# Last stage of a four-stage transformer kernel: the next steps' first norms, transposes and first projections in other units

## The chip, the cores and the metric

The kernel runs on one core of one Trainium2 chip. The metric is the device time in microseconds (us), lower is better. The engines named below are PE (matmul), DVE (vector), ACT (scalar and activation functions), POOL (GpSimd) and SP (which here only issues transfers). Each has a queue of its own and works through it strictly in program order; semaphores tie them together.

## What is computed (reference)

Sixteen images of 113 tokens with 192 features go through four stages; the last two matter here. The third is an attention with eight heads and two groups. The last one is this block, cut to what matters:

```python
e  = gelu(ln(x, r_ln) @ r_in_w.T + r_in_b)           # router
g  = mean(e[:, 1:, :], axis=1, keepdims=True)
h1 = gelu(concat([e, broadcast(g)]) @ r_o1_w.T + r_o1_b)
h2 = gelu(h1 @ r_o2_w.T + r_o2_b)
bits = argmax(h2 @ r_o3_w.T + r_o3_b)                # two bits per token
xa = ln(x, ln1);  q, k, v = xa @ wq.T + bq, xa @ wk.T + bk, xa @ wv.T + bv
o  = softmax(q k^T / 4) v, 12 heads;  o = o @ wo.T + bo
h  = x + bits[:, :, 0:1] * o
ff = gelu(ln(h, ln2) @ fc1_w.T + fc1_b) @ fc2_w.T + fc2_b
out = h + bits[:, :, 1:2] * ff
out = out + (one of three low-rank maps of out, chosen by the bits)
```

## The kernel before, in words

All data are float32. `ffn1_phase` works in four steps of four images (`G = 4`, 452 token columns). `steps` (L2142) runs the body for step 0, then a loop over steps 1 and 2 with a register as the step's number, then step 3, then a tail. A body has twelve units, one for each head. What each engine does in a unit is written out by hand in its own `body`: PE at L2299, ACT at L2402, DVE at L2660, POOL at L2487. In the body of step `it` three streams are interleaved: the attention of step `it` (scores, softmax, turn, values), the late part of step `it - 1` (names `late_...`: output projection, residual, MLP, low-rank maps), and the first part of step `it + 1` (names `pre_...`: two norms, transposes, router, q, k and v).

**The attention of a unit.** PE computes the scores of two heads ahead at even units (L2201), into two PSUM banks. DVE takes the maximum and subtracts it (`softmax_in`, L2556 and L2560), ACT takes the exp in place (L2381), PE transposes it (`turn`, L2210) and ACT copies it out (L2406). PE may compute scores for units n + 2 and n + 3 only when DVE has done the softmax input of units n and n + 1, which held the banks. Every four heads there are `values` (L2223), a copy `outputs` on ACT (L2376), a transposition `back` on PE (L2233) and `divide` on DVE (L2580, L2585).

**The first part of a step.** The first norm has no scale and is kept twice: `stat(it, 0, rows(it))` takes mean and variance of the rows in H (L2516, L2520), POOL the power of the variance (`power`, L2454), and `pre_x` (L2537) writes the norm to `xnext`. POOL copies it to `xmid` and later to `x` (`keep_mid`, `keep_last`), for the residual. `pre_stat` (L2542) and `pre_z` on DVE (L2546) norm `xnext` again into `z`. PE's `pre_z` (L1372) transposes `z` into the PSUM tiles Z1 and Z2; ACT (L1439) and DVE (`pre_z_copy`, L1483) copy them out, scaled for the router (r1, r2) and for the attention (xa1, xa2). `pre_qk(it, t)` (L1394) computes q and k of four heads, of three such parts; ACT copies q (L1457), DVE k (`pre_k`, L1497). `pre_features`, `pre_router1` and `pre_router2` (L1375 to L1392) are the router's layers, each with a Gelu on ACT; DVE's `pre_mean` (L1490) stands between the first two. ACT has to load a table whenever it goes from exp to Gelu or back.

**The order around the change.** DVE in a body: unit 0 softmax 2, `late_o`, `stat(it + 1, 0)`; unit 1 softmax 3, `late_hh`; unit 2 softmax 4, statistics of the residual, `pre_x(it + 1)`; unit 3 softmax 5, `pre_stat`, `late_y`; unit 4 softmax 6, `late_y_copy`, `pre_z`; unit 5 softmax 7, `divide`, `pre_z_copy`; unit 6 softmax 8, `pre_mean`; unit 7 softmax 9, `pre_k` 0, `late_mlp` 0; unit 8 softmax 10, `pre_k` 1, `late_mlp` 1; unit 9 softmax 11, `divide`, `late_u`; unit 10 softmax 12, `pre_k` 2, `late_down`; unit 11 softmax 13, `late_d`. Softmax 12 and 13 are those of the next step's heads 0 and 1. PE transposes `z` in unit 5, has router and feature projections of the MLP in unit 6, the three q and k parts in units 7, 8 and 10. POOL takes, in order, `power(it + 1, 0)`, `power(it - 1, 2)`, `power(it + 1, 1)`, the two copies and `out(it - 1)`, the add of the MLP's result to H.

**PSUM tiles of the first part.** The tiles Z1, Z2, R (router features), H1, H2, Q0, K0, ... V1, LG take the banks 4 and 5 in turn; a tile may be filled when the tile two before it has been copied out (`Tiles.free`). The list of readers beside them (L1321) says who copies each.

**The stage before** (`attn1_phase`, body of PE at L1755, ACT at L1857, DVE at L2015) runs, in its last step, the first part of step 0 of the last stage: PE transposes in unit 2, router layers in units 3 to 5, q and k parts in units 6 to 8.

## Time and profile before

| | us |
|---|---|
| median of 3 runs (lowest, highest) | 975.55 (973.28, 978.21) |
| the profiled execution | 979.58 |
| its span, first to last instruction | 977.8 |
| PE, DVE, ACT, POOL busy | 797.9, 495.4, 306.4, 365.4 |
| last stage, step 0 (627.4 to 686.4) | 59.0 |
| step 1 (686.4 to 765.1) | 78.6 |
| step 2 (765.1 to 843.6) | 78.6 |
| step 3 (843.6 to 903.4) | 59.8 |
| the tail, to the end of the span | 74.4 |

A step is counted from its body's first scores; the steps' limits are read from PE's timeline. Steps 1 and 2 are longer than the others because they carry all three streams. In the rows below, a line number is the kernel's line that issued the instruction (for a helper, the helper's), `x16` is how many instructions one row merges, and a bracket gives how long the engine had been idle before and on what it had waited. The granted clock is given as a share of 2.4 GHz, so 0.50 is the 1.2 GHz level and 1.00 the 2.4 GHz level.

### The profile page before, as it was taken

To read this page: it belongs to the slowest core of one execution; us is meant where nothing else is said; L and a number is where in the kernel's file an instruction comes from. 1 tells how busy PE (TensorE), PEld (TensorE's weight loads), DVE (VectorE), ACT (ScalarE), POOL (GpSimd) and SP (SyncE) were. 2 spreads that over 40 slices of the span, in tenths; PEclk is the share of its full clock that TensorE was granted. 3 is DMA by queue.
4 is the path that set the end of the run, shared out by engine and by line. 5 is a ranking of instruction groups with operands and counts; after the bars stand their busy time and mean duration, and the time that the engine had idled before them with its cause. 6 is when DMAs were issued, how large, how long until landed. Compare 5 with 4: busy or idle time off the path is not lost.

```text
span 977.8 us, 14811 instructions
## 1 busy us (share of the span) xinstructions
PE 797.9 (82%) x4860; PEld 572.6 (59%) x4860; DVE 495.4 (51%) x1223; ACT 306.4 (31%) x571; POOL 365.4 (37%) x233
## 2 busy tenths in 40 slices
PE   7988872279999999988979788779799799888572
PEld 4665662147667777756767574554656656656351
DVE  4354655524644444658676965363824743634210
ACT  1121321023333333333424337144352252342200
POOL 3015888786820287758786100010200100000000
PEclk9787765569999999997979899858789879989795
DMA  8831113334543344444111000000000000000000
GB/s 235 238 106 46 35 29 72 68 79 115 119 124 88 87 117 114 103 127 98 35 29 31 1 1 1 1 1 1 2 0 1 14 0 0 13 3 1 15 0 15
DMA packets 81395, 52.96 MB, mean 54 GB/s; under 512 B 42942, under 2 KB 76719, under 8 KB 80305
## 3 DMA queue, kind: packets, MB, share of 16 engines
q1 hardware_dynamic: 27330, 29.82, 10.9%
q0 software_dynamic: 40960, 11.98, 6.8%
q10 hardware_dynamic: 13040, 10.30, 3.7%
q8 instruction: 39, 0.64, 0.3%
q14 instruction: 26, 0.21, 0.1%
HBM read 29.53 MB, written 21.69 MB: 52 GB/s over the span
## 4 chain that ended last, share of the span: by engine, by line
PE 60%; POOL 16%; DVE 9%; issue 6%; ACT 3%; DMA 3%; SPq 0%; DVEq 0%; ACTq 0%; POOLq 0%
POOL work L223 8%; POOL xs_scratch L212 6%; PE ex_up L1143 6%; PE ex_up L1144 6%; PE ps L2270 4%; PE ps L2201 3%; PE ex_yp L1166 3%; PE ex_yp L1167 3%; PE ps L1355 2%; PE ps L1357 2%; PE ps L1350 2%; PE ps L2210 2%; PE ps L1356 2%; PE a_ps L392 1%; PE ps L1366 1%
## 5 line engine op out<-in xcount | busy, mean ns | idle before, releaser
L223 POOL DMA_INDIRECT work<-ys_scratch,place x64 | 153.8, 2403 | 87.5 <-DMA ys_scratch<-ex_yb 57.5
L212 POOL DMA_INDIRECT xs_scratch<-e_t,e_routed x64 | 152.8, 2387 | 43.0 <-issue 29.3
L1242 DVE TENSOR_SCALAR ex_bb<-ex_up 128x384 f32<-128x384 f32 x44 | 24.5, 558 | 118.6 <-PE ex_up L1144 87.7
L1143 PE MATMUL ex_up<-e_wa,ex_x 128*128 x176 | 75.1, 509 | 8.4 <-issue 6.9
L1144 PE MATMUL ex_up<-e_wb,e_ex_x 65*128 x176 | 73.9, 501 | 0.0
L2480 POOL TENSOR_TENSOR H<-H,f_hh 113x768 f32 (+1 forms) x4 | 7.2, 1810 | 146.7 <-DVE f_hh L2623 146.7
L2458 POOL TENSOR_SCALAR f_veps<-f_mv 113x4 f32<-113x4 f32 x10 | 1.9, 194 | 144.8 <-DVE f_mv L2520 144.8
L1201 ACT ACTIVATE ex_sg<-ex_up 128x384 f32<-128x384 f32 x44 | 21.6, 492 | 106.3 <-PE ex_up L1144 96.9
L2406 ACT ACTIVATE f_pT<-ps 113x452 f32<-113x452 f32 x48 | 26.2, 546 | 77.5 <-PE ps L2210 77.4
L1144 PEld LDWEIGHTS ex_up<-e_wb,e_ex_x 65*128 65x128 f32 x176 | 34.4, 196 | 24.7 <-issue 2.1
L2201 PE MATMUL ps<-f_k,f_q 32*113 32x113 f32 x384 | 32.5, 320 | 16.9 <-DVE f_p L2560 15.8
L1143 PEld LDWEIGHTS ex_up<-e_wa,ex_x 128*128 128x128 f32 x176 | 30.9, 195 | 25.7 <-issue 12.8
L1166 PE MATMUL ex_yp<-e_wa,ex_a 128*128 x176 | 43.5, 329 | 0.8 <-ACT ex_yb L1208 0.8
L1167 PE MATMUL ex_yp<-e_wb,e_ex_a 65*128 x176 | 43.3, 327 | 0.0
L2201 PEld LDWEIGHTS ps<-f_k,f_q 32*113 32x113 f32 x384 | 27.6, 221 | 22.0 <-DVE f_p L2560 15.9
L2210 PE MATMUL ps<-ident,f_p 113*113 113x113 f32 x192 | 36.8, 324 | 3.6 <-ACT f_pT L2406 3.6
L2623 DVE SCALAR_TENSOR_TENSOR f_hh<-ps,f_bits,f_hh 113x192 f32<-113x192 f32 x16 | 5.9, 413 | 64.4 <-PE ps L2270 64.4
L2381 ACT ACTIVATE f_p<-f_p 113x452 f32<-113x452 f32 x48 | 27.8, 578 | 32.9 <-DVE f_p L2560 32.5
L1126 PE MATMUL ex_xt<-ident,ex_xb 128*128 128x128 f32 x88 | 22.7, 283 | 17.7 <-DMA ex_xb<-xs_scratch 17.7
L2270 PE MATMUL ps<-fc,f_ff 128*113 128x192 f32 x192 | 36.9, 344 | 0.0
L2210 PEld LDWEIGHTS ps<-ident,f_p 113*113 113x113 f32 x192 | 28.3, 216 | 13.4 <-issue 11.9
L2556 DVE TENSOR_REDUCE f_mx<-ps 113x4 f32<-113x452 f32 x48 | 29.9, 624 | 12.0 <-PE ps L2201 10.8
(372 smaller groups left out, 1921.9 us busy)
## 6 DMA issues: line engine op xcount, KB each, us to landing
ex_xb<-xs_scratch SPq DMA_DIRECT2D x88, 96.0 KB
ys_scratch<-ex_yb ACTq DMA_DIRECT2D x44, 192.0 KB
xs_scratch<-e_zeros SPq DMA_DIRECT2D x62, 96.0 KB
e_wa<-in_wa SPq DMA_DIRECT2D x4, 1152.0 KB
e_wb<-in_wb SPq DMA_DIRECT2D x4, 576.0 KB
e_wa<-in_patches SPq DMA_DIRECT2D x4, 432.0 KB, 9.3
out<-H SPq DMA_DIRECT2D x4, 339.0 KB
w4a<-in_w4a SPq DMA_DIRECT2D x1, 1216.0 KB
```

The lines of the kernel that those rows point to most:

```text
L212: nc.gpsimd.indirect_dma_start(out=dram.xs, out_offset=bass.IndirectOffsetOnAxis(ap=S.pos[:, j, k:k + 1], axis=0), in_=S.t[:, j, :], in_of ...
L223: nc.gpsimd.indirect_dma_start(out=S.yk[:, it % 2, j, k, :], out_offset=None, in_=dram.ys[it // X.steps], in_offset=bass.IndirectOffsetOnA ...
L1143: mm(o, x1[:, p % 3, t], S.wa[:, bass.ds(w, 2 * I)], start=True, stop=False)
L1144: m = mm(o, x2[:, p % 3, t], S.wb[:, bass.ds(w, 2 * I)], start=False, stop=True)
L1166: mm(o, a1[:, p % 2, t], S.wa[:, bass.ds(w, D)], start=True, stop=False)
L1167: m = mm(o, a2[:, p % 2, t], S.wb[:, bass.ds(w, D)], start=False, stop=True)
L2201: m = mm(units.bank(h)[0:N, s], q[r:r + STRIP, h // HQ, s], k[r:r + STRIP, h // HQ, s], start=True, stop=True, tile_position=(r, 0))
L2210: m = nc.tensor.transpose(PT[0:N, j * N:(j + 1) * N], p[:, n % (AHEAD + 1), j, :], S.ident[0:N, 0:N])
L2270: m = mm(o, ff[:, f, j * N:(j + 1) * N], S.fc2[:, f, :], start=False, stop=(f == KF - 1))
L2381: cp(pp, pp, ACT.Exp, scale=float(HD) ** -0.5).then_inc(exp_ok.sem, 1)
L2406: cp(pT[:, n % 5, :, :], PT[0:N, 0:GN], ACT.Copy).then_inc(pt_out.sem, 1)
L2556: nv.tensor_reduce(mx[:, n % 2, :], sc, AX.X, ALU.max).then_inc(mx_ok.sem, 1)
```

## The change

In the last stage the two unscaled norms are made two steps ahead, later in the body. In the first body DVE makes the norms of step 1 where it made them before, and those of step 2 besides: `stat(it + 2, 0)` in unit 5, `pre_x(it + 2)` in unit 6, `pre_stat(it + 2)` in unit 8 and `pre_z(it + 2)` in unit 10. In the middle bodies only the latter stay. For step 2 they read rows of a step that does not exist; `ahead` then points at H's first rows, and the result is not used. As `z` is ready when a middle body begins, PE transposes it in unit 2 for unit 5 and computes the first q and k part in unit 3 for unit 7; ACT and DVE copy there too (DVE: `pre_z_copy` in unit 2 for 5, `pre_k` 0 in unit 3 for 7, ahead of `late_y`). In the first body the transposes stay and the first q and k part goes to unit 6, ahead of the router. The tiles Q0 and K0 take their places in the ring between Z2 and R. In the last step of the stage before, the first q and k part moves from unit 6 to unit 3, the router's three layers from units 3, 4, 5 to 4, 5, 6, and DVE's mean from unit 4 to unit 5. POOL's powers are reordered to match. The bodies of step 3 and the tail have the same instructions as before.

```diff
@@ -1318,7 +1318,7 @@
     F.z_ok, F.gm_ok, F.gs_ok = (counted(nc, ctx, "f_" + n, per) for n, per in (("z_ok", G), ("gm_ok", 1), ("gs_ok", 1)))
-    F.proj = Tiles(nc, ctx, "f_proj", S.bank[4:6], ["act", "dve", "act", "act", "act", "act", "dve", "act", "dve", "act", "dve",
+    F.proj = Tiles(nc, ctx, "f_proj", S.bank[4:6], ["act", "dve", "act", "dve", "act", "act", "act", "act", "dve", "act", "dve",
                                                     "act", "dve", "dve"])
@@ -1329,7 +1329,8 @@
     HEADS, HD, RHD = 12, D // 12, 128
-    Z1, Z2, R, H1, H2, Q0, K0, Q1, K1, Q2, K2, V0, V1, LG = range(14)
+    Z1, Z2, Q0, K0, R, H1, H2, Q1, K1, Q2, K2, V0, V1, LG = range(14)
+    QS, KS = (Q0, Q1, Q2), (K0, K1, K2)
     images, mm, P = four, nc.tensor.matmul, Names()
@@ -1392,9 +1393,9 @@
     def pre_qk(it, t):
-        pe.wait_ge(*proj.free(it, Q0 + 2 * t))
-        pe.wait_ge(*proj.free(it, K0 + 2 * t))
-        mq, mk = two_linear(proj.bank(Q0 + 2 * t)[:, 0:GN], proj.bank(K0 + 2 * t)[:, 0:GN], w.q + 128 * t, w.k + 128 * t, 128,
+        pe.wait_ge(*proj.free(it, QS[t]))
+        pe.wait_ge(*proj.free(it, KS[t]))
+        mq, mk = two_linear(proj.bank(QS[t])[:, 0:GN], proj.bank(KS[t])[:, 0:GN], w.q + 128 * t, w.k + 128 * t, 128,
                             xa1[:], xa2[:])
@@ -1455,7 +1457,7 @@
     def pre_q(it, t):
-        evac(it, proj, Q0 + 2 * t, q[:, t, :], 128, ACT.Identity, bias=col(c.q + t))
+        evac(it, proj, QS[t], q[:, t, :], 128, ACT.Identity, bias=col(c.q + t))
 
@@ -1495,9 +1498,9 @@
     def pre_k(it, t):
-        dve.wait_ge(*done(proj.filled, it, K0 + 2 * t))
-        nv.tensor_scalar(k[:, t, :], proj.bank(K0 + 2 * t)[:, 0:GN], S.c4a[:, c.k + t:c.k + t + 1], None, ALU.add
-                         ).then_inc(proj.out(K0 + 2 * t), 1)
+        dve.wait_ge(*done(proj.filled, it, KS[t]))
+        nv.tensor_scalar(k[:, t, :], proj.bank(KS[t])[:, 0:GN], S.c4a[:, c.k + t:c.k + t + 1], None, ALU.add
+                         ).then_inc(proj.out(KS[t]), 1)
 
@@ -1790,14 +1793,14 @@
                         nxt.pre_z(0, False)
-                    if n == 3 and last:
+                    if n == 4 and last:
                         nxt.pre_features(0)
-                    if n == 4 and last:
+                    if n == 5 and last:
                         nxt.pre_router1(0)
-                    if n == 5 and last:
+                    if n == 6 and last:
                         nxt.pre_router2(0)
-                    if n in (6, 7, 8) and last:
-                        nxt.pre_qk(0, n - 6)
+                    if n in (3, 7, 8) and last:
+                        nxt.pre_qk(0, max(0, n - 6))
                     if n in (2, 8):
@@ -1881,14 +1884,14 @@
                         nxt.pre_z(0)
-                    if n == 3 and last:
+                    if n == 4 and last:
                         nxt.pre_features(0)
-                    if n == 4 and last:
+                    if n == 5 and last:
                         nxt.pre_router1(0)
-                    if n == 5 and last:
+                    if n == 6 and last:
                         nxt.pre_router2(0)
-                    if n in (6, 7, 8) and last:
-                        nxt.pre_q(0, n - 6)
+                    if n in (3, 7, 8) and last:
+                        nxt.pre_q(0, max(0, n - 6))
                 outputs(it, 1)
@@ -2056,10 +2059,10 @@
                         nxt.pre_z_copy(0)
-                    if n == 4 and last:
+                    if n == 5 and last:
                         nxt.pre_mean(0)
-                    if n in (6, 7, 8) and last:
-                        nxt.pre_k(0, n - 6)
+                    if n in (3, 7, 8) and last:
+                        nxt.pre_k(0, max(0, n - 6))
                 if not last:
@@ -2190,8 +2194,8 @@
                 if n % HQ == 0:
-                    pe.wait_ge(*proj.copied(it, Q0 + 2 * (n // HQ)))
-                    pe.wait_ge(*proj.copied(it, K0 + 2 * (n // HQ)))
+                    pe.wait_ge(*proj.copied(it, QS[n // HQ]))
+                    pe.wait_ge(*proj.copied(it, KS[n // HQ]))
                 pe.wait_ge(*units.free(it, n))
@@ -2309,16 +2313,16 @@
                         late_y(it - 1)
-                    if n == 5 and not last:
+                    if n == (5 if first else 2) and not last:
                         pre_z(it + 1)
+                    if n == (6 if first else 3) and not last:
+                        pre_qk(it + 1, 0)
                     if n == 6:
...
                                 (pre_features, pre_router1, pre_router2)[m](it + 1)
-                    if n == 7 and not last:
-                        pre_qk(it + 1, 0)
                     if n == 7 and not first:
@@ -2412,8 +2416,10 @@
                         outputs(it, 0)
-                    if n == 5 and not last:
+                    if n == (5 if first else 2) and not last:
                         pre_z(it + 1)
+                    if n == (6 if first else 3) and not last:
+                        pre_q(it + 1, 0)
                     if n == 6:
@@ -2421,8 +2427,6 @@
                                 (pre_features, pre_router1, pre_router2)[m](it + 1)
-                    if n == 7 and not last:
-                        pre_q(it + 1, 0)
                     if n == 8 and not last:
@@ -2485,17 +2489,19 @@
             def body(it, first, last):
-                if not last:
+                if first:
                     power(it + 1, 0)
-                if not first:
+                    power(it + 1, 1)
+                else:
                     power(it - 1, 2)
-                if not last:
-                    power(it + 1, 1)
                 keep_last(it)
...
                     keep_mid(it + 1)
+                    power(it + 2, 0)
                 if not first:
                     out(it - 1)
+                if not last:
+                    power(it + 2, 1)
 
@@ -2534,10 +2540,10 @@
 
-            def pre_x(it):
+            def pre_x(it, src):
 
                 dve.wait_ge(*done(xmid_ok, it, -1))
-                norm(it, 0, rows(it), xnext, x_ok)
+                norm(it, 0, src, xnext, x_ok)
 
@@ -2658,6 +2664,8 @@
             def body(it, first, last):
+                if not last:
+                    ahead = rows(2 if first else (STEPS - 1) * (2 - it))
                 for n in range(NU):
@@ -2665,40 +2673,51 @@
                         late_o(it - 1)
-                    if n == 0 and not last:
+                    if n == 0 and first:
                         stat(it + 1, 0, rows(it + 1))
...
                         stat(it - 1, 2, hh)
-                    if n == 2 and not last:
-                        pre_x(it + 1)
-                    if n == 3 and not last:
+                    if n == 2 and first:
+                        pre_x(it + 1, rows(it + 1))
+                    if n == 3 and first:
                         pre_stat(it + 1)
+                    if n == 2 and not (first or last):
+                        pre_z_copy(it + 1)
+                    if n == 3 and not (first or last):
+                        pre_k(it + 1, 0)
                     if n == 3 and not first:
...
                         late_y_copy(it - 1)
-                    if n == 4 and not last:
+                    if n == 4 and first:
                         pre_z(it + 1)
+                    if n == 5 and first:
+                        pre_z_copy(it + 1)
                     if n == 5 and not last:
-                        pre_z_copy(it + 1)
+                        stat(it + 2, 0, ahead)
+                    if n == 6 and first:
+                        pre_k(it + 1, 0)
                     if n == 6 and not last:
                         pre_mean(it + 1)
-                    if n == 7 and not last:
-                        pre_k(it + 1, 0)
+                        pre_x(it + 2, ahead)
                     if n == 7 and not first:
...
                         late_mlp(it - 1, 1)
+                    if n == 8 and not last:
+                        pre_stat(it + 2)
                     if n == 9 and not first:
...
                         late_down(it - 1)
+                    if n == 10 and not last:
+                        pre_z(it + 2)
                     if n == 11 and not first:
```

## Rows read from the trace of the kernel before

**Rows 1.** The page's part 4, the chain that ended last, whole kernel.

```profile
PE 60%; POOL 16%; DVE 9%; issue 6%; ACT 3%; DMA 3%; SPq 0%; DVEq 0%; ACTq 0%; POOLq 0%
```

**Rows 2.** Windows of steps 0 and 1: length, busy us by engine, PE clock, DMA share, GB/s.

```profile
627.00:686.00 59.00, 47.70 (x331) 31.20 (x331) 30.91 (x73) 23.73 (x40) 4.91 (x7) 0.68 0.00 1
...
699.00:717.00 18.00, 16.57 (x106) 12.25 (x106) 12.18 (x30) 8.24 (x14) 2.81 (x4) 0.56 0.01 1
```

**Rows 3.** Timeline of step 1, PE and one ACT row; columns: start us, us.

```profile
686.42 1.05 PE L2201 MATMUL ps<-f_k,f_q 32*113 32x113 f32 x16
...
694.83 0.62 PE L2210 MATMUL ps<-ident,f_p 113*113 113x113 f32 x4 [0.73 <-ACT f_pT L2406]
699.61 1.86 PE L2201 MATMUL ps<-f_k,f_q 32*113 32x113 f32 x16 [4.16 <-DVE f_p L2560]
...
712.58 1.74 PE L1355 MATMUL ps<-work,w4a 128*128 128x452 f32 x2
...
716.30 1.17 ACT L1434 ACTIVATE f_ff<-ps,c4a 128x452 f32<-128x452 f32 x2 [0.92 <-PE ps L1358]
...
718.11 1.03 PE L1355 MATMUL ps<-work,w4a 128*128 128x452 f32 x2
...
726.81 1.03 PE L1355 MATMUL ps<-f_xa,w4a 128*128 128x452 f32 x2 [0.28 <-ACT f_h L1434]
...
729.48 0.57 PE L2268 MATMUL ps<-fc2b,ones 1*113 1x192 f32 x2
...
747.69 1.05 PE L2201 MATMUL ps<-f_k,f_q 32*113 32x113 f32 x16
...
758.13 0.58 PE L1366 MATMUL ps<-w4a,work 128*113 128x192 f32 x2 [0.43 <-DVE work L2644]
```

**Rows 4.** Timeline of step 1, DVE.

```profile
689.47 1.12 DVE L2516 BATCH_NORM_STATS2 f_stats<-H 113x6 f32 x4
...
691.03 0.60 DVE L2556 TENSOR_REDUCE f_mx<-ps 113x4 f32<-113x452 f32 x1
...
697.11 1.25 DVE L2526 TENSOR_SCALAR e_x<-H,f_mv,f_rstd 113x192 f32 x4
698.27 0.62 DVE L2556 TENSOR_REDUCE f_mx<-ps 113x4 f32<-113x452 f32 x1
...
710.00 0.74 DVE L1486 TENSOR_SCALAR f_r<-ps,c4b 64x452 f32<-64x452 f32 x1 [1.35 <-PE ps L1350]
...
712.18 0.63 DVE L2556 TENSOR_REDUCE f_mx<-ps 113x4 f32<-113x452 f32 x1
...
745.17 0.63 DVE L2556 TENSOR_REDUCE f_mx<-ps 113x4 f32<-113x452 f32 x1 [0.24 <-DVE f_hh L2623]
```

**Rows 5.** Timeline of step 3, PE and, last, DVE.

```profile
843.62 1.05 PE L2201 MATMUL ps<-f_k,f_q 32*113 32x113 f32 x16
...
855.14 1.86 PE L2201 MATMUL ps<-f_k,f_q 32*113 32x113 f32 x16 [2.58 <-DVE f_p L2560]
...
861.95 0.69 PE L2233 MATMUL ps<-ident,f_ot 128*113 128x128 f32 x4 [0.74 <-ACT f_ot L2376]
...
853.74 0.60 DVE L2556 TENSOR_REDUCE f_mx<-ps 113x4 f32<-113x452 f32 x1
```

**Rows 6.** Timeline of step 0, PE.

```profile
654.19 1.74 PE L1336 MATMUL ps<-f_r,w4a 128*128 128x452 f32 x2
...
666.02 1.41 PE L1355 MATMUL ps<-f_xa,w4a 128*128 128x452 f32 x2
```

**Rows 7.** Timeline of the attention stage's last step, ACT, then PE.

```profile
601.70 1.28 ACT L1434 ACT_TABLE_LOAD   x1
602.99 0.63 ACT L1434 ACTIVATE f_h<-ps,c4a 64x452 f32<-64x452 f32 x1
...
603.77 1.00 PE L1355 MATMUL ps<-f_xa,w4a 128*128 128x452 f32 x2 [0.95 <-ACT f_h L1434]
...
611.02 1.00 PE L1355 MATMUL ps<-f_xa,w4a 128*128 128x452 f32 x2 [0.33 <-DVE f_k L1499]
```

More of the change, by code:

```diff
@@ L1428, in ffn1_pre_scalar @@
     HEADS, HD, RHD = 12, D // 12, 128
-    Z1, Z2, R, H1, H2, Q0, K0, Q1, K1, Q2, K2, V0, V1, LG = range(14)
+    Z1, Z2, Q0, K0, R, H1, H2, Q1, K1, Q2, K2, V0, V1, LG = range(14)
+    QS, KS = (Q0, Q1, Q2), (K0, K1, K2)
     images, cp, P = four, nc.scalar.activation, Names()
@@ L1476, in ffn1_pre_vector @@
     HEADS, HD, RHD = 12, D // 12, 128
-    Z1, Z2, R, H1, H2, Q0, K0, Q1, K1, Q2, K2, V0, V1, LG = range(14)
+    Z1, Z2, Q0, K0, R, H1, H2, Q1, K1, Q2, K2, V0, V1, LG = range(14)
+    QS, KS = (Q0, Q1, Q2), (K0, K1, K2)
     images, nv, P = four, nc.vector, Names()
@@ L2113, in ffn1_phase @@
         units = Tiles(nc, ctx, "f_units", bank[0:2], ["dve"] * NU)
-        Z1, Z2, R, H1, H2, Q0, K0, Q1, K1, Q2, K2, V0, V1, LG = range(14)
+        Z1, Z2, Q0, K0, R, H1, H2, Q1, K1, Q2, K2, V0, V1, LG = range(14)
+        QS, KS = (Q0, Q1, Q2), (K0, K1, K2)
         O1, O2, WO, Y1, Y2, F, FO, U1, U2, DN, D1, D2, UP = 0, 1, 2, 4, 5, 6, 12, 14, 15, 16, 18, 19, 20
```

## The prediction, made before the change was run

> **What bounds the kernel now.** I read the page's chain of waits first, then the last stage by windows, then PE, DVE and ACT of one middle step in order of time. PE holds 60% of the chain [rows 1]; in the last stage it is busy most of the time, but at two clocks. A middle step (step 1, 686.4 to 765.1) has 18 us in which PE is 16.57 us busy at a mean granted clock of 0.56, that is nearly all at the 1.2 GHz level; the rest of it is at 2.4 GHz, step 2 repeats it, and in step 0 the mean clock is 0.68 [rows 2]. The low stretch begins in a hole of PE's work: 0.73 us before the turn of unit 3, then 4.16 us before the scores of heads 6 and 7, released by DVE [rows 3]. DVE is the cause: in units 0 to 3 it carries the previous step's residual and statistics and, for the next step, statistics, a first norm and second statistics [rows 4]. The change takes just these out of units 0 to 3 and gives PE work for the hole.
>
> **Middle steps (1 and 2), units 0 to 3.** Out of DVE's way before softmax 5 go the statistics at unit 0 (689.47 to 691.03, 1.56 us) and the norm at unit 2 (697.11 to 698.27, 1.16 us) [rows 4]. The first comes through only in part, since DVE then waits for PE's products. Step 3 has neither: there softmax 5 starts 10.12 us after the step's first scores (853.74 less 843.62, [rows 5]), in step 1 11.85 us (698.27 less 686.42, [rows 3, 4]). So both are worth 1.7 us. In comes the copy of the transposed norm, 710.00 to 712.18, 2.2 us with its hand-over [rows 4]. In step 1's times it ends at about 698.7, and softmax 5 (a maximum and a subtraction of 0.63 us each) at 699.95: the scores of heads 6 and 7 are free no earlier than at 699.61 now. The stall is filled, not shortened. PE runs the 8 transposes (0.95 us), then waits from 695.5 to 698.7, 3.2 us, for the copy, then runs the first q and k projection: 2.67 us at full clock (726.81 to 729.48, [rows 3]), some 5.1 us at the low one, my estimate by doubling.
>
> Queued behind: DVE's k copy now waits for PE inside unit 3, with the late norm (1.16 us as the other) and softmax 6 behind it. ACT's q copy has behind it only a copy that waits for a later turn of PE anyway.
>
> **Does the clock still fall?** Step 3 has a hole of 2.58 us and falls too, from before its scores at 855.14 (1.86 us) until before 861.95 (0.69 us) [rows 5]. My 3.2 us lies between 2.58 and 4.16, both of which fell, so I take the fall. What follows differs: in step 1 the clock came back only during the feature projections at 712.58, 1.74 us long where their like at 718.11 take 1.03 [rows 3]. Now a projection of the same kind stands right behind the hole. I take a low stretch of about 7 us, as in step 3; its ends are none and today's 15 to 17 us.
>
> With 7 us: projection to 703.8, scores and turn to 705.4, late norm ready at 705.9, its transposes and the values to 707.8, copy, back and turn to 710.3, scores and turn of unit 6 to 711.8, against 712.58 now. Then ACT is late next: softmax 7, divide, the new statistics (1.56 us) and softmax 8 end at 713.6, then an exp, the table load of 1.28 us [rows 7] and two Gelus of 1.17 us together [rows 3] end at 716.7, when the second pair of feature projections may start, now at 718.11 [rows 3]: 1.4 us gained. Unit 7 loses the projection, from the turn's end (726.81 less 0.28) to 729.48 [rows 3]: 3.0 us.
>
> **What comes back on DVE.** The second statistics (1.56 us) stand before softmax 11, which now starts at 745.17 [rows 4]; it ends near 748.05, and the scores now at 747.69 [rows 3] wait 0.4 us. The second norm (1.16 us) stands between the down product and the copy for which PE's last up-projection waits, now until 758.13 [rows 3]; 1.6 us with the 0.4. The norm at unit 6 and the statistics at unit 5 cost nothing beyond the delay of softmax 8 above: PE's router and projections hide them; without that cover they are 1.16 and 1.56 us. POOL's power for the second norm stands behind its add to H, but unit 10 comes 8 us later. Per middle step: 1.4 + 3.0 - 1.6 = 2.8 us gained; 5.2 if the clock holds (features start at 709.2, their second pair at 714.3: 3.8 + 3.0 - 1.6); -0.7 if the low stretch lasts as now (features at 715.5, so 2.1 lost there). Twice 2.8 is 5.6 us.
>
> **Step 0** does two steps' norms, 5.4 us of DVE more, in units 5 to 10. Most hides; the statistics at unit 8 delay softmax 11 and PE's scores by 1.0 us. PE's projection moves from 666.02, where it took 3.1 us, ahead of the features at 654.19, in the low stretch [rows 6]: 5.1 us there if the clock stays low, and the features then wait 0.75 us for ACT's q copy, since they now share its PSUM bank. If the clock comes back during the projection, the features (1.74 us for a pair at the low clock, [rows 6]) and the router run at full clock and the step gains 1.8 net; if not it loses 2.9. I take 0.5 lost. Step 2's norms for a step that does not exist are in the 1.6. **Step 3** and the tail have no moved work: nothing.
>
> **The attention stage's last step.** The projection moves ahead of the router there too. DVE's k copy now blocks softmax 6, and the last router layer goes to unit 6, where ACT runs a table load, an exp and a load again before it can free the bank of the next projection. Each load is 1.28 us, and at 603.77 PE waits 0.95 us for that result today; by my order it waits 2.2 us there, and the third projection starts at 612.05, now at 611.02 [rows 7]: 1.0 us lost. The bounds are 0 (other work covers it) and 2.7 (the new holes of 1.7 and 2.2 us let the clock fall once).
>
> The Trainium skill, in "ScalarE: Activation LUTs", section What ACT_TABLE_LOAD costs, gives a switch 1.283 us of load and some 1.38 us of drain besides. The load agrees: begun at 601.70 it ends before the activation of 602.99 [rows 7], which starts right behind it, so a drain has no room. By the page the two switches in that wait would make it 2.8 us longer and the sum that much worse; I go by the rows.
>
> **Sum.** -5.6 + 0.5 + 1.0, and 1.7 for one clock fall in a new hole (in the attention stage, or before the up-projection in two steps, each about even). A fall costs between nothing and 3.4 us, half of step 3's 6.8 us from 855.14 to 861.95 [rows 5]; I take the middle. That is -2.4 us. The profiled execution took 979.58 us, so 977.2 on its terms; it stands 4.0 above the median of the runs, 975.55, from which I get 973.2.
>
> The Trainium skill, in "TensorE: Matmul & The Clock Gate", Part 1, says that the place of the clock's rise varies from run to run and that the ramp is under 1% of a typical kernel. Here the rows disagree in size: 16.57 us busy at 0.56 [rows 2] is some 7 us per middle step, 14 us or 1.5% in two. By the page's size (a) and (b) would have no price of their own, and the sum would stay near -2.4.
>
> **Rivals.** (a) The filled hole keeps PE at 2.4 GHz. For it: the hole is 1 us shorter than now. Against: step 3's 2.58 us. Price: 2 x 5.2 + 1.8 - 1.0 = 11.2 us, 964.4. Chance 0.17.
> (b) Slower: in unit 3 DVE waits for a projection at the low clock, with the late norm and softmax 6 behind, and the clock does not return before the features. From a low stretch of some 13 us on, this decides. For it: transposes and scores without a pause did not bring the clock back in step 1. Price: 2 x 0.7 + 2.9 in step 0 + 2.7 in the attention stage = 7.0 us, 982.6. Chance 0.18.
> (c) The DVE work moved to units 8 and 10 takes back what the hole gave, by a clock fall before each up-projection: 2 x 1.7 more, 976.6. Chance 0.10, and it is no change.
> My forecast has 0.55. Its own range is 967 to 978.
>
> **Numbers.** A measurement of this kernel can tell 0.5%, 4.9 us. Faster by more: all of (a) and three in ten of the forecast, 0.33. Slower by more: most of (b) and a little of the forecast, 0.18. The rest, 0.49, is no change. The range takes in most of (a) and of (b): 964.5 to 981.
>
> **What would show it.** Right: PE's hole at unit 3 is about 3 us, the scores of heads 6 and 7 start over 3 us later than now, the low stretch of steps 1 and 2 is about 7 us, the steps last about 76 us for 78.6, PE waits some 1.5 us for DVE before the up-projection. Wrong: a clock that never falls there (a), a low stretch until the features (b), a step 0 that changes by over 3 us, or an attention stage that ends earlier.

## The result, and the profile after

| | before | after |
|---|---|---|
| median of 15 runs each, us | 976.45 | 982.4 |
| lowest, highest | 963.67, 986.38 | 971.17, 991.78 |
| span of the profiled execution | 977.8 | 981.7 |

The ratio is 1.0077, interval [1.0039, 1.0114]: slower, where I had forecast 973.2 with a range up to 981.0. The same kernel was timed twice more: 1.0009 [0.9953, 1.0064] (e4_same) and 1.0040 [1.0013, 1.0068] (e12_same_again). The mean of the three is 1.0042, about 4 us slower. A median is over all executions of a kernel, while the ratios leave out the slow ones, those over 1.5% above the kernel's fastest, which is why e5_fill_mid can have a median of 982.17 us and a ratio below 1.

The view by windows, cut where the work changes: from the transposes of the attention stage's last step to the last stage's first scores, then steps 0, 1, 2, then step 3 with the tail. Columns: stretch and length, busy us (and instructions) of PE, PE's weight loads, DVE, ACT, POOL, then PE's granted clock, DMA share, GB/s. Before:

```profile
582.25:627.40 45.15, 35.99 (x260) 22.89 (x259) 19.95 (x37) 23.07 (x34) 0.00 (x0) 0.96 0.00 1
627.40:686.42 59.02, 48.12 (x334) 31.57 (x334) 31.19 (x73) 23.73 (x40) 4.91 (x7) 0.68 0.00 1
686.42:765.05 78.63, 70.40 (x479) 47.87 (x478) 40.33 (x101) 28.02 (x48) 7.02 (x9) 0.89 0.01 1
765.05:843.62 78.57, 70.35 (x480) 47.87 (x479) 40.32 (x101) 28.02 (x48) 7.04 (x9) 0.89 0.01 4
843.62:977.80 134.18, 87.72 (x557) 60.95 (x556) 40.33 (x95) 28.68 (x48) 6.83 (x7) 0.83 0.03 8
```

And after:

```profile
584.90:637.75 52.85, 41.56 (x260) 26.48 (x259) 19.85 (x37) 23.18 (x34) 0.00 (x0) 0.84 0.00 1
637.75:699.49 61.74, 49.13 (x335) 32.59 (x335) 36.25 (x97) 23.72 (x40) 7.30 (x11) 0.70 0.00 1
699.49:773.90 74.41, 65.69 (x479) 43.15 (x478) 40.01 (x101) 27.76 (x48) 7.02 (x9) 0.98 0.01 2
773.90:848.43 74.53, 65.84 (x479) 43.16 (x478) 39.99 (x101) 27.77 (x48) 7.01 (x9) 0.98 0.01 5
848.43:981.70 133.27, 87.10 (x557) 60.43 (x556) 40.18 (x95) 28.65 (x48) 6.80 (x7) 0.83 0.03 8
```

Read the lengths against each other: the attention stage's last step is 7.70 us longer, step 0 2.72 longer, steps 1 and 2 4.22 and 4.04 shorter, step 3 with the tail 0.91 shorter: +1.25 us together. The remaining 2.65 of the span's 3.9 us lie ahead of the transposes (582.25 to 584.90), where both kernels have the same instructions. The clock column says more: with two levels, a stretch of length L at mean clock c has been at 1.2 GHz for 2 x (1 - c) x L. This is called its low time from here on. In a middle step that was 17 us and is 3 us; in the attention step it was 4 us and is 17 us.

Step 1 after, PE, in order of time; it answers [rows 3]:

```profile
699.49 1.05 PE L2205 MATMUL ps<-f_k,f_q 32*113 32x113 f32 x16
...
707.00 0.94 PE L1351 MATMUL ps<-ident,e_z 113*128 113x113 f32 x8
707.89 0.62 PE L2214 MATMUL ps<-ident,f_p 113*113 113x113 f32 x4
711.66 1.88 PE L1356 MATMUL ps<-f_xa,w4a 128*128 128x452 f32 x2 [3.15 <-DVE f_xa L1491]
...
715.84 1.05 PE L2205 MATMUL ps<-f_k,f_q 32*113 32x113 f32 x16
...
723.27 0.94 PE L1356 MATMUL ps<-work,w4a 128*128 128x452 f32 x2
...
728.30 1.02 PE L1356 MATMUL ps<-work,w4a 128*128 128x452 f32 x2 [0.47 <-ACT f_ff L1436]
...
736.65 0.58 PE L2272 MATMUL ps<-fc2b,ones 1*113 1x192 f32 x2
...
755.45 1.05 PE L2205 MATMUL ps<-f_k,f_q 32*113 32x113 f32 x16 [0.52 <-DVE f_p L2566]
...
766.98 0.58 PE L1367 MATMUL ps<-w4a,work 128*113 128x192 f32 x2 [1.52 <-DVE work L2650]
```

The middle step is as drawn in the prediction. PE waits 3.15 us for DVE's copy (forecast 3.2), the projection starts at the low clock (1.88 us for 1.03 in [rows 3]), the scores of heads 6 and 7 come 16.35 us into the step for 13.19 before, and DVE's returned work makes PE wait 0.52 and 1.52 us. But the clock is back within the projection, after 3.4 us and not 7.

The attention stage's last step after, ACT and then PE; it answers [rows 7]:

```profile
606.74 0.55 ACT L1848 ACTIVATE a_ot<-ps 128x452 f32<-128x452 f32 x1 [2.09 <-PE ps L1719]
607.31 1.28 ACT L1436 ACT_TABLE_LOAD   x1
608.60 0.64 ACT L1436 ACTIVATE f_h<-ps,c4a 128x452 f32<-128x452 f32 x1
609.14 0.54 ACT L1864 ACTIVATE a_pT<-ps 113x452 f32<-113x452 f32 x1
609.69 1.28 ACT L1842 ACT_TABLE_LOAD   x1
610.99 0.58 ACT L1842 ACTIVATE a_p<-a_p 113x452 f32<-113x452 f32 x1
611.58 1.28 ACT L1436 ACT_TABLE_LOAD   x1
612.88 0.63 ACT L1436 ACTIVATE f_h<-ps,c4a 64x452 f32<-64x452 f32 x1
```

```profile
610.36 0.65 PE L1693 MATMUL ps<-ident,a_p 113*113 113x113 f32 x4
613.66 1.84 PE L1356 MATMUL ps<-f_xa,w4a 128*128 128x452 f32 x2 [2.65 <-ACT f_h L1436]
...
619.73 1.00 PE L1356 MATMUL ps<-f_xa,w4a 128*128 128x452 f32 x2
```

PE's second projection waits 2.65 us for the Gelu of the last router layer (forecast 2.2), because ACT goes through load, Gelu, copy, load, exp, load, Gelu in strict order. The clock falls in that hole, so it takes 6.07 us from this projection to the next, where 3.63 are needed before (607.39 to 611.02).

### The profile page after: what moved, and what is told of

Read it like the earlier page. It is cut to its first block, busy times and chain, and to the rows that moved or that the text cites. A ratio compares the mean times of both kernels' runs of the same rounds, so it can differ in the third digit from the quotient of the medians.

```text
span 981.7 us, 14847 instructions
## 1 busy us (share of the span) xinstructions
PE 796.8 (81%) x4860; PEld 569.1 (58%) x4860; DVE 499.4 (51%) x1247; ACT 306.1 (31%) x571; POOL 367.2 (37%) x237
## 4 chain that ended last, share of the span: by engine, by line
PE 65%; DVE 14%; POOL 8%; issue 6%; ACT 3%; DMA 2%; SPq 0%; DVEq 0%; ACTq 0%; POOLq 0%
POOL xs_scratch L212 6%; PE ex_up L1143 6%; PE ex_up L1144 6%; PE ps L2274 3%; PE ex_yp L1166 3%; PE ex_yp L1167 3%; PE ps L2205 3%; PE ps L1634 3%; PE ps L1356 2%; PE ps L1358 2%; PE ps L1357 2%; PE ps L1674 2%; PE ps L1613 2%; DVE H L236 1%; PE a_ps L392 1%
## 5 line engine op out<-in xcount | busy, mean ns | idle before, releaser
L1144 PE MATMUL ex_up<-e_wb,e_ex_x 65*128 x176 | 71.9, 489 | 0.0
L2205 PE MATMUL ps<-f_k,f_q 32*113 32x113 f32 x384 | 30.0, 303 | 10.2 <-DVE f_p L2566 9.2
L2214 PE MATMUL ps<-ident,f_p 113*113 113x113 f32 x192 | 34.7, 310 | 2.2 <-ACT f_pT L2410 2.2
L1674 PE MATMUL ps<-a_k,a_q 32*113 32x113 f32 x256 | 21.6, 308 | 16.8 <-DVE a_p L1960 16.8
L2205 PEld LDWEIGHTS ps<-f_k,f_q 32*113 32x113 f32 x384 | 25.5, 205 | 15.7 <-DVE f_p L2566 8.0
```

The source lines that it names most:

```text
L1144: m = mm(o, x2[:, p % 3, t], S.wb[:, bass.ds(w, 2 * I)], start=False, stop=True)
L1674: return mm(units.bank(n)[0:N, c], q[r:r + STRIP, t, c], k[r:r + STRIP, t, c], start=True, stop=True, tile_position=(r, 0))
L2205: m = mm(units.bank(h)[0:N, s], q[r:r + STRIP, h // HQ, s], k[r:r + STRIP, h // HQ, s], start=True, stop=True, tile_position=(r, 0))
L2214: m = nc.tensor.transpose(PT[0:N, j * N:(j + 1) * N], p[:, n % (AHEAD + 1), j, :], S.ident[0:N, 0:N])
```

## Experiments

Lengths are given in the order of the windows above (attention step / step 0 / step 1 / step 2 / rest). The kernel before has 45.15 / 59.02 / 78.63 / 78.57 / 134.18, the kernel after 52.85 / 61.74 / 74.41 / 74.53 / 133.27.

**e1_attn_old.** The kernel after, with the attention stage's last step in the order of before.

```diff
-                    if n in (3, 7, 8) and last:
-                        nxt.pre_qk(0, max(0, n - 6))
+                    if n in (6, 7, 8) and last:
+                        nxt.pre_qk(0, n - 6)
```

(The router's layers, the copies and the tiles' order of step 0 likewise.)

> The changed kernel with the order of the kernel before in the attention stage's last step (router layers in units 3 to 5, first projection in unit 6); the last stage keeps the change. Theory A (the loss sits in the attention stage: the router's last layer is pushed behind ACT's exps and table loads, and the new holes let PE's clock fall): from the transposes in unit 2 to the last stage's first scores 45 to 47 us instead of 52.85; the kernel 5 to 8 us shorter than the changed one, so 0 to 4 us below the kernel before. Rival B (most of the 7.7 us is where the clock happened to fall, at 588 us, before any moved instruction ran): the stretch shrinks by 2 us or less in its order and stays near 50 us. Rival C (the change's loss is in the last stage's step 0): the kernel stays 4 us or more above the one before.

Measured: 974.54 us, ratio 0.9962 [0.9925, 0.9999]; 43.66 / 60.96 / 80.42 / 75.63 / 137.78. Without the new order in the attention stage the change is no longer slower. The attention step is even 1.5 us shorter than before (45 to 47 us expected), at a clock of 1.00 throughout: its hole of 2.54 us, behind which the clock was low for 3.5 us before, let it stay up. The profiled execution is the slowest of the twelve (984.03 us), and its five stretches add up to 2.9 us more than before, although the runs say 3.7 us less. Steps 1 and 2 run the same instructions and differ by 4.79 us:

```profile
688.47:768.89 80.42, 72.60 (x480) 48.03 (x479) 40.30 (x101) 27.77 (x48) 7.02 (x9) 0.87 0.01 1
768.89:844.52 75.63, 67.39 (x480) 43.87 (x479) 39.99 (x101) 27.87 (x48) 7.02 (x9) 0.95 0.01 5
```

In step 1 the clock fell in the hole of unit 3 and came back only after 20.5 us. In step 2 it was low twice for about 3.4 us, within the projection behind the hole (from 781.9) and at the first feature projections (from 792).

**e2_attn_new.** The reverse: the kernel before, with the new order in the attention stage's last step alone.

```diff
-                    if n in (6, 7, 8) and last:
-                        nxt.pre_qk(0, n - 6)
+                    if n in (3, 7, 8) and last:
+                        nxt.pre_qk(0, max(0, n - 6))
```

> The kernel before with the changed order in the attention stage's last step alone. Theory A: the stretch from the transposes to the last stage's first scores grows from 45.15 to 50 to 53 us, and the kernel is 5 to 8 us (0.5 to 0.8 percent) slower than the one before. Rival B: 1 to 3 us slower. The steps of the last stage keep their 59, 78.6, 78.6 us.

Measured: 986.02 us, ratio 1.0097 [1.0052, 1.0141]; 52.92 / 57.80 / 75.70 / 75.69 / 138.39. The new order costs the attention step the same 7.8 us here, and the kernel is 9.5 us slower, more than I had expected. Steps 1 and 2 are the code of before, with its hole of 4.16 us. I had expected them to keep their 78.6 us; they take 75.7, because the clock came back after 7 us (0.95 for 0.89). The second pair of feature projections then starts 28.76 us into the step, where it started after 31.69 us before:

```profile
724.98 1.03 PE L1365 MATMUL ps<-work,w4a 128*128 128x452 f32 x2 [0.86 <-ACT f_ff L1449]
```

**e3_middle_only.** The kernel after, with the orders of before in the attention stage and for the first q and k part of step 0; what is left of the change is the norms two steps ahead and units 2 and 3 of steps 1 and 2.

```diff
-                    if n == (6 if first else 3) and not last:
+                    if n == 3 and not (first or last):
                         pre_qk(it + 1, 0)
...
+                    if n == 7 and first:
+                        pre_qk(it + 1, 0)
```

> The changed kernel with the old order in the attention stage and, in the last stage's step 0, the first projection behind the router again; the norms two steps ahead and the moved transposes and projections of the middle steps stay. Theory: steps 1 and 2 take 74.5 us each for 78.6, step 0 takes 60 us (59.0 before, 1.0 for the statistics ahead of softmax 11), so the kernel is 6 to 8 us faster than the one before. Rival C (step 0's order costs nothing by itself, its 2.7 us are the norms' on DVE): step 0 stays at 61.7 us and the kernel equals the run with the attention stage alone restored.

Measured: 976.77 us, ratio 0.9973 [0.9941, 1.0004]; 45.13 / 61.17 / 74.56 / 75.65 / 137.70. My expectation (steps of 74.5 us, step 0 of 60 us, 6 to 8 us faster than before) held for step 1 alone; the kernel cannot be told from the one before. Step 0 is 2.15 us longer than before with PE's order of before: in this kernel its cost is DVE's, not PE's. DVE, ACT and PE of this kernel's step 0:

```profile
647.31 1.14 DVE L2549 BATCH_NORM_STATS2 f_stats<-H 113x6 f32<-113x192 f32 x4
648.59 0.38 DVE L2553 BATCH_NORM_AGGREGATE f_mv<-f_stats 113x2 f32<-113x6 f32 x4
648.88 0.60 DVE L2589 TENSOR_REDUCE f_mx<-ps 113x4 f32<-113x452 f32 x1
```

```profile
650.18 0.58 ACT L2410 ACTIVATE f_p<-f_p 113x452 f32<-113x452 f32 x1 [1.68 <-DVE f_p L2593]
650.77 1.28 ACT L1467 ACT_TABLE_LOAD   x1
652.07 0.64 ACT L1467 ACTIVATE f_e<-ps,c4a 128x452 f32<-128x452 f32 x1
```

```profile
653.62 1.87 PE L1399 MATMUL ps<-f_e,ro 128*128 128x452 f32 x2 [2.37 <-DVE f_gs L1518]
```

The statistics of unit 5 stand ahead of softmax 8; its exp stands ahead of the router's Gelu on ACT; PE's router waits 2.37 us, 1.59 before. The last stretch (step 3 and the tail), in which nothing was moved, is 3.5 us longer than before, at a clock of 0.79 for 0.83.

**e4_same.** The kernel after, unchanged.

> The changed kernel unchanged, beside the others on the same chip: 4 to 10 us slower than the one before. The parts that no clock fall touches last as in the first profile (steps 1 and 2 with 74.4 and 74.5 us); if the clock's falls move, the attention stretch moves from 52.85 us to anything between 47 and 53.

Measured: 977.85 us, ratio 1.0009 [0.9953, 1.0064]; 52.94 / 61.78 / 74.44 / 74.53 / 133.34. The 4 to 10 us of loss that I had expected did not show: the interval reaches from 4.6 us faster to 6.3 us slower. Every stretch agrees with the first profile within 0.1 us, yet the span is 972.8 for 981.7 us: the whole 8.9 us lie ahead of the transposes, which start at 575.77 for 584.90. In all profiles but one they start between 575.77 and 585.50, whatever the kernel; in e11_attn_fill3 they start at 601.58.

**e5_fill_mid and e6_fill_before.** Is it the clock that costs the time in the hole of unit 3? e5 is e3 with 7 matmuls of no use there in steps 1 and 2, e6 is the kernel before with 10 of them.

```diff
                     turn(it, n)
+                    if n == 3 and not (first or last):
+                        pe.wait_ge(*late.free(it - 1, Y1))
+                        fill(late.bank(Y1), 10)
```

> As e3_middle_only, with seven dummy matmuls (128 x 452, results never read) on PE behind the turn of unit 3 in the two middle steps, to keep PE busy in the hole before the moved projection. Clock theory (the hole of 3.15 us makes the granted clock fall once; the projection behind it brings it back): no low stretch at unit 3, the projection at 2.67 us, steps of 72 to 73.5 us against 74.56 and 75.65; 2 to 5 us in two steps. Rival (the work order sets the time, DVE's chain ends last and a faster projection only waits): steps within 0.5 us of 74.5.

> The kernel before with ten such dummy matmuls in the same place of the middle steps, where its hole of 4.2 us is. Clock theory (what the change gains in the middle steps is mostly the clock, 17 us at the low level before against 3.4 us after): the low stretch goes, and steps fall from 78.6 (75.7 in another execution) to 72 to 74 us, as short as with the change. Rival (the gain is PE's work moved into the hole): steps stay over 75 us.

Measured: e5 982.17 us, ratio 0.9953 [0.9905, 1.0002]; 43.66 / 62.96 / 74.81 / 75.90 / 137.66. e6 980.64 us, ratio 1.0038 [1.0001, 1.0075]; 45.16 / 59.06 / 77.06 / 77.06 / 134.20. The clock stays up in the hole (1.00 in both steps of e6), but both clock theories are missed: no step comes near 72 to 74 us. The steps of e5 are no shorter than those of e3 (74.56 and 75.65). PE of e6:

```profile
697.84 7.76 PE L2239 MATMUL ps<-w4a 128*128 128x452 f32 x20
705.53 1.05 PE L2201 MATMUL ps<-f_k,f_q 32*113 32x113 f32 x16
```

One such matmul is issued as two and takes 0.78 us; ten of them hold the scores back to 16.55 us into the step, 3.4 us later than before. So the fillers themselves took time that the clock had given back, up to those 3.4 us per step. The runs show that the clock can be held, but not its price.

**e7_attn_fill and e11_attn_fill3.** The kernel after, with 6 and with 3 such matmuls before the attention step's second projection.

```diff
         pe.wait_ge(*proj.free(it, QS[t]))
+        if isinstance(it, int) and it == 0 and t == 1:
+            for _ in range(3):
+                mm(proj.bank(QS[t])[:, 0:GN], S.w4a[:, 0:128], S.w4a[:, 0:GN], start=True, stop=True)
```

> The changed kernel with six dummy matmuls in the attention stage's last step, ahead of the second projection, where PE waits 2.65 us for ACT. If the clock is most of the loss there: from the transposes to the last stage's first scores 48 to 50 us against 52.9, with the low stretch behind the wait gone. If the order is most of it (ACT's queue of exps and table loads ahead of the router's last layer): 51 us or more.

> The kernel after with 3 matmuls of no use before the second projection of the attention stage's last step, where e7_attn_fill had 6 (4.73 us, which ended 1.9 us after ACT had freed the bank). Theory (of the 7.7 us that this stretch grew by, about 2.3 us are the new order's waits and the rest is time at the low clock): the clock stays high as in e7_attn_fill, the projection starts when ACT's h2 is done, and the stretch from the transposes to the last stage's first scores takes 47 to 48 us (45.15 before, 52.85 after, 49.19 with 6). Rival (the order itself costs 4 us, whatever PE does in the hole): it stays at 49 us or more. If 3 matmuls are too few the clock falls in the remaining 1 us and the stretch takes 51 us or more.

Measured: e7 979.61 us, ratio 1.0026 [0.9988, 1.0064]; 49.19 / 61.50 / 74.29 / 74.54 / 133.21. e11 978.25 us, ratio 0.9985 [0.9953, 1.0017]; 49.96 / 61.95 / 72.91 / 74.53 / 133.27. PE of e11:

```profile
601.58 0.94 PE L1351 MATMUL ps<-ident,e_z 113*128 113x113 f32 x8
...
626.29 2.45 PE L1399 MATMUL ps<-w4a 128*128 128x452 f32 x6
629.01 1.02 PE L1356 MATMUL ps<-f_xa,w4a 128*128 128x452 f32 x2 [0.27 <-ACT f_h L1439]
...
632.66 1.00 PE L1356 MATMUL ps<-f_xa,w4a 128*128 128x452 f32 x2 [0.33 <-DVE f_k L1505]
...
645.17 0.91 PE L1747 MATMUL ps<-w1w,a_out 96*113 96x192 f32 x2 [0.23 <-DVE a_out L2002]
645.88 0.85 PE L1748 MATMUL ps<-w1w,a_out 97*113 97x192 f32 x2
```

With the hole filled the clock holds there and the third projection starts 31.08 us after the transposes, against 28.77 before and 34.83 after: 2.3 us is the price of the new order itself, the rest is clock. For e7 the 48 to 50 us expected came (49.19); e11's 47 to 48 us did not (49.96), since the clock fell later, at 645.2, ahead of output projections behind a wait of only 0.23 us (0.85 us each for 0.49), a place where it holds in the kernel before. PE had waited 1.29 and 0.94 us in the 8 us ahead of it, but so it had before. The fall and what follows it are the other 2.5 us that this step is longer than before.

**e8_z_late.** e3 with the second norm for step `it + 2` behind `late_d` in unit 11, for unit 10.

```diff
-                    if n == 10 and not last:
-                        pre_z(it + 2)
                     if n == 11 and not first:
                         late_d(it - 1)
+                    if n == 11 and not last:
+                        pre_z(it + 2)
```

> As e3_middle_only, with DVE's second norm for the step after next behind the copy for the up-projection (unit 11) and not ahead of softmax 13 (unit 10). Theory (the 1.52 us that PE waits for DVE before its last up-projection are this norm): the wait falls to 0.3 to 0.6 us and each middle step is 1.0 to 1.2 us shorter than in e3 at equal clock. Rival (DVE is then late with the v copy or the router bits): no gain.

Measured: 978.01 us, ratio 0.9964 [0.9919, 1.0009]; 45.13 / 61.17 / 73.46 / 71.80 / 134.01. PE ahead of the last up-projection of step 1:

```profile
757.67 0.58 PE L1377 MATMUL ps<-w4a,work 128*113 128x192 f32 x2 [0.43 <-DVE work L2677]
```

The wait is 0.43 us again, as in [rows 3], for 1.53 in e3, and step 1 is 1.10 us shorter, as expected: the norm's 1.1 us was a real price and avoidable. Step 2 shows a granted clock of 1.00: in the same hole of 3.15 us the clock did not fall, and the step is 1.66 us shorter than step 1, whose projection starts like after's.

**e9_best and e10_best_fill.** e8 with the first norm of step 0 in unit 7 and the second statistics in unit 10, where DVE waits for PE; e10 has 5 fillers in unit 3 besides.

```diff
+                    if n == (7 if first else 6) and not last:
                         pre_x(it + 2, ahead)
...
-                    if n == 8 and not last:
-                        pre_stat(it + 2)
...
                     if n == 10 and not last:
+                        pre_stat(it + 2)
                         pre_k(it + 1, 2)
```

> The kernel of e8_z_late (old order in the attention stage and in step 0, second norm in unit 11) with two more moves on DVE: in step 0 the first norm for step 2 goes from unit 6 to unit 7, and in all steps the second statistics go from unit 8 to unit 10, in both cases ahead of a copy for which DVE waits for PE anyway (6.34 us and 3.3 us idle there in step 0). Theory (the 2.1 us that step 0 grew by in e3_middle_only are 0.8 us of a longer wait before the router, 2.37 for 1.59, and 1.3 us of statistics ahead of softmax 11): step 0 is back at about 59.1 us, the 0.52 us wait before the scores of unit 9 in steps 1 and 2 goes, and from the transposes of the attention stage's last step on the kernel takes 383 to 388 us, 395.6 in the kernel before; ratio to it 0.987 to 0.995. Rival (what one wait gives up the next takes, or the clock's phase takes): step 0 stays at 61 us and the ratio is 0.996 or above. Against both: the second norm may wait for POOL's power in unit 11, since its statistics are now only a unit ahead; then the wait before the last up-projection grows from 0.43 to 1.5 us or more.

> e9_best with 5 matmuls of no use (256 to 452 columns of idle weights into a free bank) in the hole of unit 3 of steps 1 and 2, where the 7 of e5_fill_mid held the clock at its high level but took as long as they saved. If the clock's fall in that hole costs what e8_z_late shows (73.46 us with 3.4 us at the low level, 71.8 us with none), steps 1 and 2 take about 71.8 us each and the kernel is up to 1.7 us per step faster than e9_best. If low clock time costs little there because PE waits for DVE and ACT right behind anyway, the steps stay within 0.5 us of those of e9_best.

Measured: e9 973.54 us, ratio 0.9978 [0.9943, 1.0012]; 46.60 / 60.30 / 72.82 / 73.65 / 137.67. e10 965.96 us, ratio 0.9891 [0.9846, 0.9936]; 46.36 / 58.44 / 72.79 / 71.60 / 133.92, from the transposes on 383.1 us for 395.6. e10 is faster than the kernel before, by 1.1% (with six executions measured), and so than the kernel after. For e9 my expectation was missed: 391.0 us from the transposes on for 383 to 388, step 0 at 60.3 us for 59.1, and a ratio on the rival's side of 0.996. In both the wait of 0.52 us in unit 9 is gone. The expected gain before the router did not come: that wait is still 2.37 us in e10, since its cause is the statistics of unit 5 (shown under e3), which I had not moved. Of the fillers: step 1 of e10 does not differ from e9's (72.79 and 72.82), since its clock fell at 690.2, ahead of the hole that they fill, and was low there for some 3 us. Step 2 is 2.05 us shorter (clock 1.00 for 0.95). Step 0 and the last stretch, with no edit between e9 and e10, are 1.86 and 3.75 us shorter:

```profile
761.78:833.38 71.60, 67.67 (x490) 44.45 (x489) 40.16 (x101) 27.79 (x48) 7.02 (x9) 1.00 0.02 5
833.38:967.30 133.92, 87.70 (x557) 61.19 (x556) 40.23 (x95) 28.68 (x48) 6.79 (x7) 0.83 0.03 8
```

So 5.6 of the 7.9 us between these two profiles lie where nothing was edited. Whether e10's lead over e9 is the fillers' doing or luck of the clock's place is open.

The second pair of feature projections of step 2 of e9, where the new order had 6.8 us of low time behind its hole, starts 29.73 us into the step:

```profile
790.71 1.03 PE L1366 MATMUL ps<-work,w4a 128*128 128x452 f32 x2 [0.44 <-ACT f_ff L1451]
```

**e12_same_again.** The kernel after once more.

> The kernel after, unchanged, once more: its two measurements so far are 1.0077 [1.0039, 1.0114] and 1.0009 [0.9953, 1.0064]. If the changed part alone decides (396.8 and 397.0 us from the transposes of the attention stage's last step on, in two profiles, against 395.6 before), the ratio is 1.001 to 1.004 and the profile again has 52.9, 61.8, 74.4 and 74.5 us for that step, step 0, step 1 and step 2, each within 0.3 us unless the clock falls in another place. If the 6 us of the first measurement are real and lie upstream of the change, the ratio is 1.006 or more with the same 397 us behind the transposes.

Measured: 981.16 us, ratio 1.0040 [1.0013, 1.0068]; 52.92 / 61.76 / 74.42 / 74.53 / 133.31. Three profiles of this kernel have the same stretches within 0.1 us, 396.8 to 397.0 us in all, clock falls included. The expectation held. So for this kernel the clock's place behind the transposes came out the same in three executions. What moves it between kernels is not shown. It is not only the code ahead of it: e3 and e5 have the same instructions up to unit 3 of step 1, and yet 45.13 and 43.66 us in the attention step and 61.17 and 62.96 in step 0.

## Why the prediction was wrong

**The attention stage's last step: the step that failed.** I had +1.0, and a clock fall for 1.7 us at even chance with the up-projections' holes: at most 2.7. It costs 7.7 to 7.8 us, three times with the rest of the change and once alone (e2). By the rows of the third projection, 28.77 to 34.83 us after the transposes: 2.3 us are the order (e11), about 1.3 are a low stretch of 6.8 us for 3.5 ahead of the first projection, behind a hole of 2.54 us that both kernels have, and 2.4 us are the second projection at the low clock (6.07 for 3.63). Another 1.6 us come behind the third, where the clock falls once more at 632.8.

Two things went wrong. The order's term was too small: my wait was 2.2 for 2.65 us, and I overlooked that ACT's copy `outputs` (606.74) now stands ahead of the router's first Gelu and waits 2.09 us for PE's values, which delays the whole chain of loads. (This is read from the rows; no run moved that copy.) And I priced a fall of the clock by the 6.8 us of step 3 [rows 5] at 1.7 us, once; there are 13 us more of low clock in this step, in three places. So the term that failed is the +1.0 with its outer bound of 2.7: what stands in its place is 2.3 us of order and 5.4 of clock. None of my signs of being wrong covered it: an attention stage that ends later was not among them.

**Step 0.** I had +0.5, with an outer bound of +2.9; it is +2.7. PE before, then after, at the second q and k projection and behind it:

```profile
670.55 0.94 PE L1355 MATMUL ps<-f_xa,w4a 128*128 128x452 f32 x2
...
673.13 0.99 PE L2223 MATMUL ps<-f_pT,f_v 113*32 113x113 f32 x32
```

```profile
672.74 1.02 PE L1387 MATMUL ps<-f_e,ro 128*128 128x452 f32 x2 [1.59 <-DVE f_gs L1498]
...
681.28 1.74 PE L1356 MATMUL ps<-f_xa,w4a 128*128 128x452 f32 x2
...
685.22 0.99 PE L2227 MATMUL ps<-f_pT,f_v 113*32 113x113 f32 x32
...
688.95 1.05 PE L2205 MATMUL ps<-f_k,f_q 32*113 32x113 f32 x16 [0.91 <-DVE f_p L2566]
```

Up to this projection the step is 0.4 us later than before (43.53 us in, for 43.15): the wait of the router features on a shared bank, 0.81 us (forecast 0.75), came, and so did the return of the clock in the first projection, which gave part of it back. The projection itself then takes 3.94 us to the values for 2.58, because the clock fell again from 673.7 to 684: 1.4 us that I had no term for. No net low time was saved (mean clock 0.70 for 0.68, low time 37.5 us in both). The statistics at unit 8 make the rest, with a wait of 0.91 us (forecast 1.0). The statistics at unit 5 stay hidden here, as I had said: the router waits 1.59 us in both kernels. In the order of e3 they do not, and cost 0.8 us.

**Steps 1 and 2.** I had -2.8 each; they gave -4.2 and -4.0. Hole, fall and DVE's two waits were right to 0.1 us. The low stretch was 3.4 us, not 7, and I had set the new order's 7 against the old order's 17, though the old order can have 7 as well (e2). Of the -4.2 in step 1, -2.9 had come by the second pair of feature projections (28.81 us into the step for 31.69), where I had -1.4; -3.0 came in unit 7, as forecast; and +1.7 came back from DVE's later work (forecast 1.6). The first of these is the clock's and not the order's: the old order gets there in 28.76 us when the clock is low for 7 us (e2), and the new order in 29.73 when it is low for 6.8 behind its hole (step 2 of e9), 1.0 later. So filling the hole costs 1.0 us at that low time, unit 7 gives 3.0, DVE takes 1.7, and some 0.3 us are left.

Whole steps say the same. The old code takes 78.6 us with 17.1 us low and 75.7 with 7 (e2); the new one 80.4 with 20.5 and 75.6 with 6.8 in two parts (e1), 74.4 with 3.4, and 72.9 with none (step 1 of e11). At about 7 us low both take the same time to 0.1 us. In equal low time the new order of the middle steps is thus worth less than 0.5 us in these few instances, until the second norm and statistics are moved out of PE's way (e8, e9: 1.1 and 0.5 us per step). Whether the new order makes the low time short is not shown: the old code had 7 us of it in e2, and the new code 20.5 in e1.

**The sum.** -2.4 forecast; by the windows +1.25 in the changed part, and +2.65 ahead of it in the first pair of profiles, of which I had no term, since nothing is changed there. By the timed runs it is about +4 us, between +0.9 and +7.5 by measurement. The span and the mean clock of single executions, 110 of the kernel before and 39 of the kernel after, say more. Within either kernel an execution is longer by some 0.33 us for each us of low time more (correlation 0.86 and 0.91), so most of the spread from execution to execution goes with the clock. The mean span is 976.0 us before and 979.0 after, 3.0 us apart with about 1.9 us of uncertainty, which the windows' 1.25 just fits. And the mean low time, worked out as above for whole spans, is 276 and 274 us: the 15 us less that the two profiles show behind the transposes do not show on average. They are in part luck of the pair: the profile of before had 284 us of it, 7 more than its kernel's mean.

Two workings of the prediction were off besides. A projection of 2.67 us doubles to 5.3 us, not 5.1. And "under 1%" of this kernel is anything up to 9.8 us, so it did not take the price from (a) and (b).

**The rivals.** (a) priced a held clock at 5.2 us per middle step. It was held in step 1 of e11, whose code there is that of after, and the step took 72.91 us, 5.7 less than before: the price was about right, and the case came by chance of place, once with this code and once in e8. Most of it is had already with the 3.4 us fall, which costs 1.5 us (74.41 to 72.91) to 1.7 (e8). (b) ended on the right side, by the wrong mechanism: the clock does not stay low until the features in the middle steps of after. It did in step 1 of e1, which took 80.4 us, 1.8 more than before where I had priced 0.7. Its term for the attention stage (2.7) was the one that came, three times as large. (c), falls before the up-projections, did not happen: with waits of 1.52 us there the step's whole low time is 3.4 us and lies at unit 3.

**The price of the clock.** The low time behind the transposes is about 120 us before and 105 after (2 x (1 - c) x L summed over the windows), and the same code of a middle step differs by 7.5 us between none and 20.5 us of it. An estimate from the 0.33 us per us above and the mean low time of 276 us is some 90 us for the whole kernel, 9% of it. The Trainium skill, in "TensorE: Matmul & The Clock Gate", Part 1, puts the ramp under 1% of a typical kernel. The trace does not agree with that size for a kernel in which the clock falls again and again. The same section's sentence that the place of the rise varies from run to run is not borne out behind the transposes of this kernel, where three executions agree; between kernels with the same instructions ahead the place does vary (e3 and e5).

## What to carry to other kernels

Before moving work past an activation that needs another table, write out the in-order queue of that engine with every load and every copy that waits for someone else: the wait that results is the sum of the chain, and here it opened a 2.65 us hole that also cost the matmul engine its clock. Compare schedules of a matmul-bound loop at equal granted clock, and over several instances of the same code: one profile's 4 us can be the clock's and not the order's. Where every execution lists its mean clock, a plot of time against it is the cheapest check of which it is. Small vector work that is moved off one wait should go where its engine is idle for another engine anyway, and everything behind it in the queues, the activation engine's too, has to be followed.

## What was not expected of the hardware

The same hole of 3.15 us, ahead of the same instructions, let the clock fall in most steps and not in others (step 2 of e8, step 1 of e11), and the hole of 2.54 us in the attention step did in the kernel before and not in e1 and e5; and in e11 it fell at 645.2 right behind a wait of only 0.23 us. What follows a fall is as uneven: 3.4, 6.8, 17.1 or 20.5 us at the low level behind holes of 2.5 to 4.2 us. Yet three executions of one kernel agree in all of it within 0.1 us per stretch, even with 9 us of difference ahead of them. A table load took 1.28 us in every row shown, and where its input was there the next activation began right behind it (607.31 and 1.28 us, then 608.60), so the drain that the prediction weighed and set aside does not show in the new chain of loads either.
